# A new order of work on four engines in a two-layer attention and feed-forward kernel, with six PSUM banks for the first projections

## What is computed

```python
qkv = jnp.einsum('btc,ec->bte', x, Wqkv) + bqkv
q, k, v = jnp.split(qkv, 3, axis=-1)
q = jax.nn.elu(q * scale) + 1.0        # per head of 16 channels
k = jax.nn.elu(k * scale) + 1.0
k_cumsum = jnp.cumsum(k, axis=1)       # over the tokens
kv_cumsum = jnp.cumsum(k * v, axis=1)
denom = jnp.clip(jnp.einsum('bthd,bthd->bth', q, k_cumsum), EPS, None)[..., None]
y = q * kv_cumsum / denom
x = layernorm(x + (y @ Wproj.T + bproj))
h = gelu(quant(x) @ quant(w_fc).T + b_fc)          # 256 -> 1024
x = layernorm(x + (quant(h) @ quant(w_proj).T + b_proj))
```

## Time and profile before

| what | us |
|---|---|
| median of 3 runs | 321.66 (320.56 to 325.51) |
| the profiled execution | 322.44 |
| its span in the profile | 320.7 |
| TensorE matmul busy | 267.6 (83%), 1460 instructions |
| VectorE busy | 255.1 (80%), 505 instructions |
| ScalarE busy | 169.1 (53%), 278 instructions |
| GpSimd busy | 159.5 (50%), 113 instructions |

### The profile page before, as it was taken

One profiled execution on the slowest core, in us unless ns is written; L12 is line 12 of the kernel. 1 busy time (PEld: TensorE's weight loads), 2 busy tenths in 40 slices (PEclk: granted clock), 3 DMA queues, 4 the chain that ended last, 5 costly groups with the idle time before them and its releaser, 6 DMA issues.

```text
span 320.7 us, 4268 instructions
## 1 busy us (share of the span) xinstructions
PE 267.6 (83%) x1460; PEld 166.6 (52%) x1476; DVE 255.1 (80%) x505; ACT 169.1 (53%) x278; POOL 159.5 (50%) x113
## 2 busy tenths in 40 slices
PE   5798965599899988999899989998999896778670
PEld 5435632276547554756466645655566454544450
DVE  2477745837979998899889988998899889867922
ACT  0543315335563856485657565755576457246332
POOL 0035242525364836473656455655575466466611
PEclk9579998758999999999999999999999999979877
DMA  6900002000100120011001010012002000200011
GB/s 180 345 1 3 0 1 65 1 0 2 65 0 2 65 66 2 1 67 31 34 2 55 16 64 0 24 43 65 2 0 67 1 0 1 67 0 2 0 65 65
DMA packets 13556, 11.82 MB, mean 37 GB/s; under 512 B 3040, under 2 KB 13280, under 8 KB 13536
## 3 DMA queue, kind: packets, MB, share of 16 engines
q1 hardware_dynamic: 11904, 11.28, 10.8%
q10 hardware_dynamic: 1632, 0.27, 0.5%
HBM read 7.35 MB, written 4.19 MB: 36 GB/s over the span
## 4 chain that ended last, share of the span: by engine, by line
DVE 57%; PE 25%; issue 6%; ACT 4%; DMA 3%; POOL 3%; SPq 0%; ACTq 0%; POOLq 0%; DVEq 0%
PE abank L900 11%; DVE h_amax L718 10%; DVE stats L692 7%; DVE hq L629 7%; PE dbank L964 4%; DVE kvsum L670 4%; DMA h<-in_L_ffn_w_fc_dram 3%; DVE kf L653 3%; DVE h_pow L621 3%; DVE r L686 3%; DVE r L730 2%; DVE ksum L665 2%; PE bbank L932 2%; DVE x_amax L708 2%; DVE kv L660 2%
## 5 line engine op out<-in xcount | busy, mean ns | idle before, releaser
L900 PE MATMUL abank<-xT,WqkvT 128*128 128x512 f32 x192 | 98.6, 642 | 21.3 <-DVE kf L653 17.2
L326 POOL TENSOR_TENSOR h_round<-h,h_inv 128x1024 f16<-128x1024 f32 x32 | 64.6, 2017 | 18.9 <-DVE h_inv L624 17.6
L900 PEld LDWEIGHTS abank<-xT,WqkvT 128*128 128x128 f32 x192 | 35.4, 201 | 59.5 <-issue 27.2
L436 ACT ACTIVATE h<-hbank 128x512 f32<-128x512 f32 x64 | 37.5, 597 | 35.2 <-PE hbank L950 34.9
L311 POOL TENSOR_TENSOR rstd<-vareps,minus_half 128x4 f32<-128x4 f32 x16 | 17.4, 1090 | 56.7 <-DVE vareps L704 56.7
L950 PE MATMUL hbank<-w_fcT,xqT 128*128 128x512 bf16 x128 | 40.3, 398 | 2.9 <-ACT w_prT L485 1.1
L302 POOL TENSOR_TENSOR qk<-qf,ksum 128x512 f32<-128x512 f32 x16 | 23.8, 1489 | 35.1 <-DVE ksum L665 29.4
L718 DVE TENSOR_REDUCE h_amax<-h 128x32 f32<-128x1024 f32 x32 | 38.7, 1208 | 1.7 <-ACT h L436 1.7
L430 ACT ACTIVATE expz<-abank,zbias_neg 128x512 f32<-128x512 f32 x32 | 22.0, 688 | 32.4 <-PE abank L900 32.4
L446 ACT COPY hT<-tbank 128x512 uint32<-128x512 uint32 x32 | 18.6, 581 | 33.3 <-PE tbank L957 33.3
L964 PE MATMUL dbank<-w_prT,hT 128*128 128x256 bf16 x256 | 35.8, 286 | 0.0
(11 more groups left out here) (90 smaller groups left out, 427.4 us busy)
## 6 DMA issues: line engine op xcount, KB each, us to landing
x_sb<-in_L_attn_x_dram SPq DMA_DIRECT2D x8, 512.0 KB, 3.6
out_dram<-o_sb SPq DMA_DIRECT2D x7, 512.0 KB, 2.9
h<-in_L_ffn_w_fc_dram SPq DMA_DIRECT2D x1, 1024.0 KB, 10.1
h<-in_L_ffn_w_proj_dram SPq DMA_DIRECT2D x1, 1024.0 KB, 11.3
Wqkv_sb<-in_L_attn_Wqkv_dram SPq DMA_DIRECT2D x1, 512.0 KB, 6.6
out_dram<-o_sb SPq DMA_DIRECT2D x4, 128.0 KB, 1.7
Wqkv_sb<-in_L_attn_Wqkv_dram SPq DMA_DIRECT2D x1, 256.0 KB, 6.8
Wproj_sb<-in_L_attn_Wproj_dram ACTq DMA_DIRECT2D x1, 256.0 KB, 7.1
```

What stands on the lines that cost most here:

```text
L326: nc.gpsimd.tensor_tensor(h_round[:, t % 2].rearrange("p (g j) -> p g j", j=BLOCK_K), h[:, t].rearrange("p (g j) -> p g j", j=BLOCK_K), h_ ...
L436: nc.scalar.activation(h[:, t, half * HALF:(half + 1) * HALF], hbank[half][:, :], ACT.Gelu).then_inc(s_h, 1)
L900: last = nc.tensor.matmul(ps[:, :], WqkvT[:, k, e * P:(e + 1) * P], xT[:, k], start=(k == 0), stop=(k == CC - 1))
```

## The change

The lists of all four engines are rewritten; the operations are the same. In the start:

- The six projections of chunk 0 go to six banks: k to `abank` 0 and 1, q to `hbank` 0 and 1, v to `tbank` and `dbank`. Wproj is turned (through `tbank`) between the two halves of x, and has semaphores of its own.
- VectorE splits the biases before it looks at the weights' exponents.
- For chunk 1 the projection of q (c = 0) stands ahead of chunk 0's output projections, and the weights w_fc are turned later.
- `up` of chunk 0 waits for two of the four turned weight pieces instead of four.

The repeated part is cut at another place of the cycle: `step(s)` is called for s = 0 to 4 and handles chunk s's last tiles, chunk s+1's feed-forward and chunk s+2's attention, and turns x of chunk s+3. A written-out copy for chunks 5 to 7 and a tail follow.

```diff
-        def run(step):
-
-            for i in range(ROUNDS - 1):
-                step((2 * i + 2, 0), (2 * i + 1, 1), (2 * i, 0))
-                step((2 * i + 3, 1), (2 * i + 2, 0), (2 * i + 1, 1))
+        STEPS = 5
...
             def copy_wprojT():
-                act.wait_ge(s_wT_ps, 4)
-                nc.scalar.copy(WprojT[:, :, :], tbank[:, :].rearrange("p (c n) -> p c n", c=CC)).then_inc(s_wT, 1)
+                act.wait_ge(s_wproj_ps, 1)
+                nc.scalar.copy(WprojT[:, :, :], tbank[:, :].rearrange("p (c n) -> p c n", c=CC)).then_inc(s_wprojT, 1)
...
+            split_biases()
             w_exponents(0)
-            split_biases()
             feature(0, 1, 0, abank[0])
+            sum_k(0, 0, 0)
             feature(0, 1, 1, abank[1])
-            sum_k(0, 0, 0)
-            feature(0, 0, 0, abank[0])
-            feature(0, 0, 1, abank[1])
+            feature(0, 0, 0, hbank[0])
             sum_k(0, 0, 1)
+            feature(0, 0, 1, hbank[1])
+            multiply_kv(0, 0, tbank)
+            multiply_kv(0, 1, dbank)
...
                 if isinstance(n, int) and n == 0:
-                    pe.wait_ge(s_w16, 4)
+                    pe.wait_ge(s_w16, 2)
                     pe.wait_ge(s_brow, 9 * 16)
...
             transpose_x(0, 0, 0, abank[0])
+            transpose_wproj()
             pe.wait_ge(s_wT, 2)
             transpose_x(0, 0, 1, abank[1])
-            pe.wait_ge(s_xT, 1)
             project(0, 1, 0, abank[0])
-            pe.wait_ge(s_xT, 2)
             project(0, 1, 1, abank[1])
+            project(0, 0, 0, hbank[0])
+            project(0, 0, 1, hbank[1])
+            pe.wait_ge(s_wprojT, 1)
+            project(0, 2, 0, tbank)
+            project(0, 2, 1, dbank)
             pe.wait_ge(s_f[1], 1)
-            project(0, 0, 0, abank[0])
+            transpose_x(1, 1, 0, abank[0])
             pe.wait_ge(s_f[1], 2)
...
+            project(1, 1, 0, abank[0])
+            transpose_rec(0, 0)
+            transpose_rec(0, 1)
+            project(1, 0, 0, abank[1])
+            project_out(0, 0)
+            project_out(0, 1)
+            pe.wait_ge(s_f[0], 3)
+            project(1, 1, 1, abank[1])
+            project(1, 2, 0, abank[0])
             transpose_w_fc(0)
             transpose_w_fc(1)
```

597 lines of the change are left out of this document (328 added, 269 removed).

## The result

The kernel after takes 282.3 us (281.76 to 282.59, 4 runs), the one before in the same series 322.68 (320.56 to 325.51). The ratio is 0.877 [0.871, 0.882]: faster by 12%, in the direction forecast. The profiled execution took 282.59 us with a span of 280.8, where the forecast had a span of 291.1.

A forecast was written before the change was run, and what follows sets the result against it. VectorE and TensorE taken as nearly full in a repeat, with VectorE idle at the ends. Start 68.3, five cycles of 31.1, chunk 7 at 253.3, tail 37.8: span 291.1, forecast 292 us, range 283 to 304.

The forecast's parts named there:

- The base of 28.94: Repeat: VectorE's time left of 32.77 us after taking off 1.91 of waits and 1.92 of collisions.
- the wait before `kv` (0.2): Repeat: 0.2 us of VectorE's wait for the v projection is left, since a down projection goes first.
- that of `x_amax` (0.45): Repeat: `x_amax` waits 0.45 us because chunk s+1's normalisation comes 1.6 us later than by the old order.
- that before the second `kf` (0.1): Repeat: `kf` (c=1) waits 0.1 us, as its k projection starts later by as much as `qf`.
- `kvsum` (0.75): Repeat: the first `kvsum` scan collides with GpSimd's second `qk`, costing 0.75 us.
- `ksum` (0.7): Repeat: the `ksum` (c=1) scan collides with GpSimd's `x_round`, costing 0.7 us.
- Rival 3: Scans do not collide and TensorE holds the cycle: 29.7 us a cycle, 1.0 less in the start, 283 us; chance 0.14.
- Rival 1: The repeat gains nothing, VectorE and TensorE both being nearly full: cycles of 32.77, 302 us; chance 0.17.
- The large term: Start, chunk 1: `qf`'s wait of 4.15 us goes, and chunk 0's mean and variance ends near 42.5 us.
- Here the banks buy little: Start, chunk 0's projections through six banks: a gain of about 0.6 us, since TensorE's 24 matmuls fill the time.
- The bias split: Start: splitting biases first frees VectorE for `kf` but gives only some 0.4 us, as the second k projection lasts until 20.
- Rival 2: TensorE's clock falls in the start and stays down, some 4 to 5 us of work at double time: 297 us; chance 0.10.

The follow-up runs named there:

- `shift_later`: Kernel after with four tiny GpSimd instructions between `rstd` and `shift` of the first norm; 291.57 us, ratio 0.895, a repeat 30.55 us.
- `no_up_bias`: Kernel after without the eight bias matmuls a chunk in the up projections (b_fc left out of the result); 281.24 us, ratio 0.871, a repeat 29.88 us.
- `bias_late`: Kernel after with the biases split after the weights' exponents again; 283.01 us, ratio 0.882.
- `before_warm32`: Kernel before with 32 instead of 20 warming transposes ahead of the first weights; 323.19 us, ratio 1.011.
- `before_both`: Kernel before with the biases split first and 32 instead of 20 warming transposes; 318.09 us, no ratio.
- The halves measured apart: New start with old loop and tail, 304.94 us (0.954); old start with new loop and tail, 298.67 us (0.937).

## Why the prediction was right in kind and too long

**The repeat: 31.1 forecast, 29.88 measured; 5.8 of the 10.3 us.** This is the step that failed, and by the prediction's own sign ("wrong if a repeat is over 32.3 or under 30.2") it did. The base of 28.94 holds: 28.94 and the 0.64 and 0.4 of the rows above make 29.98. Of the added terms the wait before `kv` (0.2) and that of `x_amax` (0.45) are nil, that before the second `kf` (0.1) is 0.64, `kvsum` (0.75) is some 0.4, and `ksum` (0.7) is nil; `h_pow` (0.15) is some 0.1. The sentence at fault is "then `shift` issues just as `ksum` starts. Chunk s+1's normalisation comes 1.6 us later than by the old order, and `x_amax` waits 0.45". `shift` issues 0.09 us before the scan, so the scan blocks nothing on the path, and `x_round` comes early enough to miss the second `ksum` but for 0.13 us. `shift_later` shows that the mechanism was right and that it hung on 0.1 us which way it fell: with `shift` behind the scan, `x_amax` waits 0.64 and `ksum` takes 1.93 (some 0.6 us of the delay being the pads' own). A placing by hand, whose steps are rounded to a tenth, cannot decide such a race. Both outcomes belonged in the sum with their prices, one of them at 31.1 less 0.45 and 0.7, which is 29.95.

**Rival 3 came true in its number, not in its reason, which is luck.** It gave 29.7 a repeat and 283 us. But the scans do collide where they meet GpSimd (the first `ksum` 3.05 us, `kvsum` up to 1.94), and TensorE's work as a whole does not hold the repeat (`no_up_bias`), only the stretch up to `kv`. Rival 1 is out, by 2.9 us a repeat.

**The rule of the Trainium skill, SBUF — State Buffer, "Who interferes with whom"** (of a VectorE and a GpSimd instruction that contend, the second to issue blocks), was used rightly and placed wrongly. The runs bear it out for scans: 3.05 us beside the rounding of the weights against 1.27 free, 1.93 beside `x_round`, and `h_round` 2.91 us behind a scan. But a rule for what happens on meeting says nothing on whether two instructions meet.

**The start: 68.3 forecast, 65.72 measured.** The large term was right: `qf`'s wait gone, chunk 0's mean and variance at 38.77. Three things were off. "Here the banks buy little, since TensorE's own 24 matmuls fill the time" priced them at about 0.6; they are worth 2 to 3 us. The reason given was the slow first projections of the earlier trace rows, 6.59 us, and these were not to last: at 3.67 us, as in the profile of the kernel after, TensorE runs ahead of VectorE and must wait for banks. The bias split, "some 0.4", is worth some 1.5 us in the profiles of the kernel after (`bias_late`, counted from the first projection). In the kernel before it is worth 0.4 at (1) with the first projections slow; the 2.8 us between the profiles of `before_warm32` and `before_both` are partly the low clock from 20 to 25 us of the former. And the 1.0 us "for small delays" was not needed. From one profile to the next (1) moves by up to 4.1 us with the same order, so the 2.6 us are within what one profile can tell. Rival 2 did not come: the granted clock was 1.00 from 40 us to (1).

**Chunk 6 to 7 and the tail.** The first is the repeat's error again: 29.88 less 1.46 is 28.42, with 1.57 forecast for the `h_amax` that falls out. In the tail 36.9 was right (36.99 measured), and the 0.9 us added for the low clock was not: the last down matmuls ran at 1.05 us for eight, and the granted clock was 1.00 until 270 us.

**The collision of `hq`**, 1.34 us a repeat, went as forecast, and the waits of the tail stayed. The halves measured apart support the split of the gain as well: 17.0 and 23.2 us.

**The range** failed by 0.7 us because its low end was rival 3 as a whole, and the start's errors went in the same direction as the repeat's.
